# A graph attention kernel: the gathers of a pair of batches in one run, with a wait for their landing between pairs

## The reference

```python
q = (feat @ Wq.T + bq).reshape(n, H, HD)
k = (feat @ Wk.T + bk).reshape(n, H, HD)
v = (feat @ Wv.T + bv).reshape(n, H, HD)
score = jnp.einsum('ehd,ehd->eh', q[edge_dst], k[edge_src])
score = jnp.clip(score / math.sqrt(HD), -10.0, 10.0)
...
alpha = ex / den[edge_dst]
wv = jax.ops.segment_sum(alpha[:, :, None] * v[edge_src], edge_dst, num_segments=n).reshape(n, C)
y = wv @ Wp.T + bp
x = feat + y
h = _layernorm(x, ln_g, ln_b)
h = jax.nn.gelu(h @ W1.T + b1, approximate=False) @ W2.T + b2
return x + h
```

## Time and profile before

| | us |
|---|---|
| median of 3 runs | 1454.29 (1449.91 to 1466.74) |
| the profiled execution | 1484.0 |
| TensorE busy | 1135.0 |
| VectorE busy | 954.9 |
| GpSimd busy | 912.0 |
| ScalarE busy | 672.3 |
| GpSimd idle before gathers | 443.4 |
| VectorE idle before products | 346.6 |

### The profile page before, as it was taken

One profiled execution on the slowest core, in us unless ns is written; L12 is line 12 of the kernel. 1 busy time (PEld: TensorE's weight loads), 2 busy tenths in 40 slices (PEclk: granted clock), 3 DMA queues, 4 the chain that ended last, 5 costly groups with the idle time before them and its releaser, 6 DMA issues.

```text
span 1484.0 us, 26187 instructions
## 1 busy us (share of the span) xinstructions
PE 1135.0 (76%) x6188; PEld 724.7 (49%) x6188; DVE 954.9 (64%) x1539; ACT 672.3 (45%) x1936; POOL 912.0 (61%) x1550
## 2 busy tenths in 40 slices
PE   8956778776977778777866876768877967877887
PEld 6823335454544454444544544544544544544566
DVE  6806676677676576666666666657667657666573
ACT  3212235455544545535544544535544535544543
POOL 4584667677776566766667566666667566666500
PEclk9976668999898788888798788887897788878699
DMA  9985877768777667776677676676677676676510
GB/s 328 314 253 178 254 227 225 229 199 253 214 220 225 203 188 222 227 232 196 197 237 208 191 230 197 199 236 179 206 236 209 191 238 196 197 225 199 180 54 23
DMA packets 154887, 312.25 MB, mean 210 GB/s; under 512 B 32200, under 2 KB 73126, under 8 KB 154791
## 3 DMA queue, kind: packets, MB, share of 16 engines
q0 software_dynamic: 61536, 200.85, 45.6%
q1 hardware_dynamic: 93254, 110.43, 23.3%
HBM read 270.02 MB, written 41.16 MB: 210 GB/s over the span
## 4 chain that ended last, share of the span: by engine, by line
PE 42%; another core or an unknown queue 23%; ACT 14%; issue 14%; DVE 5%; ACTq 1%; DVEq 0%; DMA 0%; SPq 0%
PE bank L483 9%; PE bank L503 7%; PE bank L951 5%; PE quad L875 4%; PE bank L930 3%; PE quad L942 3%; PE bank L977 3%; PE bank L964 2%; ACT hid L496 2%; PE bank L455 2%; ACT hid L491 1%; DVE kv L1636 1%; ACT hn L1276 1%; ACT staged L1217 1%
## 5 line engine op out<-in xcount | busy, mean ns | idle before, releaser
L401 POOL DMA_INDIRECT kv<-kv_rows,src_sb x750 | 721.5, 962 | 443.4 <-PE bank L951 212.1
L1616 DVE TENSOR_TENSOR prod<-kv,quad 128x1024 f32<-128x1024 f32 x196 | 239.3, 1221 | 346.6 <-remote 228.0
L1636 DVE TENSOR_TENSOR kv<-kv,bank 128x1024 f32<-128x1024 f32 x196 | 238.2, 1215 | 16.7 <-ACT kv L1209 16.7
L1623 DVE TENSOR_REDUCE score<-prod 128x32 f32<-128x1024 f32 x196 | 237.7, 1213 | 0.8
L483 PE MATMUL bank<-hT,w_sb 128*128 128x256 f32 x736 | 212.4, 440 | 17.9 <-ACT hid L491 17.9
L951 PE MATMUL bank<-kv,onehot 128*32 128x264 f32 x1568 | 150.1, 442 | 83.2 <-issue 49.5
L503 PE MATMUL bank<-w_sb,hid 128*128 128x256 f32 x736 | 205.3, 435 | 0.9 <-issue 0.7
L483 PEld LDWEIGHTS bank<-hT,w_sb 128*128 128x128 f32 x736 | 159.6, 222 | 52.5 <-issue 11.6
L942 PE MATMUL quad<-qwin,onehotT 32*128 32x256 f32 x1568 | 108.8, 354 | 95.7 <-issue 54.1
L503 PEld LDWEIGHTS bank<-w_sb,hid 128*128 128x128 f32 x736 | 159.8, 223 | 34.5 <-issue 8.7
L930 PE MATMUL bank<-staged,place 128*128 128x264 f32 x196 | 81.5, 502 | 113.8 <-ACT staged L1217 76.0
(11 more groups left out here) (164 smaller groups left out, 1421.0 us busy)
## 6 DMA issues: line engine op xcount, KB each, us to landing
qwin<-q_rows SPq DMA_DIRECT2D x392, 64.0 KB
dst_rows<-edge_dstT SPq DMA_DIRECT2D x50, 256.0 KB
q_rows<-q_next SPq DMA_DIRECT2D x25, 512.0 KB
kv_rows<-kv_out SPq DMA_DIRECT2D x24, 512.0 KB
kv<-kv_rows,src_sb POOLq DMA_INDIRECT x750
agg_rows<-acc_sb SPq DMA_DIRECT2D x98, 82.5 KB
xT_sb<-xT SPq DMA_DIRECT2D x25, 256.0 KB, 5.4
xq_sb<-xT SPq DMA_DIRECT2D x25, 256.0 KB
```

The lines of the kernel that those rows point to most:

```text
L401: return nc.gpsimd.indirect_dma_start(out=rows, out_offset=None, in_=kv_dram, in_offset=bass.IndirectOffsetOnAxis(ap=index, axis=0))
L1616: nc.vector.tensor_tensor(prod[:, slot % 2].rearrange("p (i c) -> p i c", c=C), kv[:, slot, :, 0:C], quad[:, :, 0:C], ALU.mult).then_inc(s ...
L1623: nc.vector.tensor_reduce(score[:, slot % 2], prod[:, slot % 2].rearrange("p (h d) -> p h d", d=HD), AX.X, ALU.add).then_inc(s_score, 1)
L1636: nc.vector.tensor_tensor(kv[:, slot, :, C:2 * C].rearrange("p i (h d) -> p i h d", d=HD), kv[:, slot, :, C:2 * C].rearrange("p i (h d) -> ...
```

## The change

The iotas behind the gathers are gone, with their tile and semaphore. The waits stand now only in front of an even batch, that is of a pair: GpSimd waits until all gathers of the two batches before have landed (`last_pair_landed`), and until both batches of the pair that held the slots have been added up. Then it issues the gathers of both batches in a row.

```diff
-            def pause(parity, t, last):
-                done = nc.gpsimd.iota(idle_rows[:, parity, t], [[1, PAUSE]], base=0, channel_multiplier=0,
-                                      allow_small_or_imprecise_dtypes=True)
-                if last:
-                    done.then_inc(s_pause, 1)
+            def last_pair_landed(turn, i):
+                for b in range(2):
+                    slot = (i - 2 + b) % SLOTS
+                    pool.wait_ge(s_kv[slot], kv_done(turn if i else turn - 1, slot))
+                    pool.sem_inc(s_gate_pool, 1)
 
             def edges(turn, r, parity):
                 for i in range(SLOTS):
...
                     if i % 4 == 0:
                         pool.wait_ge(s_src[buffer], 16 * (r + 1))
-                    if exists(n - SLOTS, BATCHES):
-                        pool.wait_ge(s_part, n - SLOTS + 1)
+                    if i % 2 == 0 and exists(n - 2, BATCHES):
+                        last_pair_landed(turn, i)
+                    if i % 2 == 0 and exists(n - SLOTS, BATCHES):
+                        pool.wait_ge(s_part, n - SLOTS + 2)
                         pool.sem_inc(s_gate_pool, 1)
-                    if exists(n - 2, BATCHES):
-                        pool.wait_ge(s_pause, n - 1)
-                        pool.sem_inc(s_gate_pool, 1)
-                    tiles = gathered(n) - len(x_tiles(turn, i))
-                    for t in range(tiles):
+                    for t in range(gathered(n) - len(x_tiles(turn, i))):
                         col = (i % 4) * TILES + t
                         gather_rows(kv[:, i, t, 0:2 * C], src_sb[:, buffer, col:col + 1]).then_inc(s_kv[i], 16)
-                        pause(i % 2, t, t == tiles - 1)
```

More of the change, by code:

```diff
@@ L17 @@
 WIN = 32
-PAUSE = 64
 WINDOW_STARTS = (0, 10, 25, 41)
@@ L161, in gnn_program @@
         onehotT = sb("onehotT", [P, 4, 2 * P], f32r)
-        idle_rows = sb("idle_rows", [P, 2, TILES, PAUSE])
         onehot = sb("onehot", [P, 4, PAIR_TILES, WIN])
@@ L264, in gnn_program @@
         s_xkvm = sem("x_rows_projected")
-        s_pause = sem("pauses_done")
         s_ohT = sem("transposed_onehots_ready")
```

## The result

The kernel after took **1478.65 us** (median; 1475.99 to 1482.76) where the kernel before took 1455.09 beside it: a ratio of 1.0248, with a 95% interval of 1.018 to 1.0316. The forecast was 1424 us and faster. The time lies inside the range given (1375 to 1482), the sign is wrong.

What follows compares the result with a forecast made beforehand. It took TensorE's signals, held up while GpSimd issues gathers, to bound the kernel. Terms -16 - 8 - 8 - 8 + 10 = -30 us took the median 1454.29 to 1424 us; own range 1395 to 1442, wider range 1375 to 1482.

Steps and rivals of the forecast that it cites:

- What bounds the kernel: No engine is full; TensorE's signals come late while GpSimd issues gathers, behind 23% unknown time (341 us) in the chain.
- The iotas go, -16 us: Inside pairs on GpSimd: 46 us less issuing at 0.35 us per us, -16 us (0 to -46).
- The wait for landing, and its floor: Between pairs on GpSimd: landing 2.1 us, waking 0.9, so a 12.3 us cycle under the present 13.6 a pair.
- The lead of 13 us as cover: Gathers start over 13 us ahead of their products, which was to cover later starts and landing waits at no cost.
- The start, -8 us: First run of 27 gathers is broken up, so first products come earlier than 115.69: -8 us (0 to -18).
- Long runs broken, -8: Runs of eleven gathers, as around 1065, can't occur any more: -8 us (0 to -20).
- fewer runs, -8: 98 runs of gathers instead of 114 to 120, each ending with up to 1 us without signals: -8 us (0 to -22).
- The wait for both batches of the old pair, 0: Even batch's gathers start 5 to 7 us later, with the odd one's slot; covered by the lead, so 0.
- Runs of eight, +10: Runs of eight gathers instead of four and four may hold signals up longer: +10 us (0 to +80).
- landing is exposed: Rival, chance 0.03: lead used up, 206 us of landing on the path less the iotas' 154: +52, 1506 us.

Runs made afterwards that it cites:

- g3: Kernel before with iotas of 256 columns instead of 64, with late signals: 1372.7 us, 0.9202 of before.
- f1: Kernel before unchanged, run again for a second profile, with prompt signals: 1152.6 us.
- D: Set of kernels measured side by side with late signals: before took 1493.5 us, four experiments 0.9202 to 0.9936 of it.
- f2: Kernel after unchanged, run again with prompt signals and profiled: 1480.47 us, 1.2863 of before.
- h1: Kernel after unchanged, run once more in another comparison with prompt signals: 1479.25 us, 1.2845 of before.
- A: The comparison that gave the result, with late signals: before 1455.1 us, after 1.0248 of it.
- e3: Kernel after with landing waits only ahead of batches 2, 4 and 6 of the first turn, prompt signals: 1113.6 us, 0.9678 of before.
- e1: Kernel after without its landing waits, with prompt signals: 1102.6 us, 0.9602 of before.
- e6: Kernel before without its iotas and the wait on them, slot wait per batch kept, prompt signals: 1098.6 us, 0.9554 of before.
- k1: Kernel after without its landing waits, with late signals: 1477.4 us, 0.9887 of before.
- g4: Kernel before without its iotas and the wait on them, with late signals: 1476.7 us, 0.9917 of before.
- F: Set measured side by side with late signals: before 1494.7 us, after 0.9935 of it, after without landing waits 0.9887.
- f3: Kernel after with its landing wait moved one pair back, to the pair before last, prompt signals: 1102.3 us, 0.9576 of before.
- B: Set of kernels measured side by side with prompt signals: before took 1150.1 us, four experiments 0.9554 to 1.3213 of it.

## Why the prediction was wrong, point by point

- **What bounds the kernel.** Right for the trace that was read: signals are late because of the gathers (g3). But their lateness is a condition of the comparison and not of the kernel (f1), and one profile could not show that.
- **The iotas go, -16 us.** Right in size with late signals, as far as D can tell: -12 to -17 us, and the interval of the ratio reaches from -7 to -18 us. The spacing is 1.26 us as taken. With prompt signals the rate is 1 us per us of issuing and not 0.35: -51.5 us.
- **The wait for landing, and its floor: the step that failed.** The prediction worked out GpSimd's own cycle as 9.3 + 2.1 + 0.9 = 12.3 us a pair, found it under 13.6, and so took the wait as hidden. Waking is 0.93 us as taken. Landing is 3.18 us (after) to 3.28 us (f2) after the end of a run of eight, not 2.1; the 2.1 were read off the DMA share after one run at the start, and a share that has fallen is not the last landing of a run in the steady state. In the trace of before the last landing recorded in a break came 2.4 us after the run (mean of the 111 breaks over 1.5 us after 130 us), so only a part of the missing 1.1 us could be read in advance. The cycle is 13.66 us. Over 98 pairs that is 133 us, and the floor of the whole kernel rises from some 1350 to 1480 us: over the 1424 forecast, and over the 1455 of before. f2 and h1 show this floor where signals are prompt (1480.5 and 1479.3 us). After took the same 1478.65 in A, and its trace there has 396.3 us of waits for landings against 19.2 for slots: GpSimd's own cycle set its pace. The comparison was also made with the profiled turns, 54.4 us, of an execution 30 us over its median; per pair the median's pace is 0.3 us less, 13.3, so even the pace to be beaten was nearer.
- **The lead of 13 us as cover.** It was there, and was spent: a cycle longer than the pace eats any lead. In the profile of after the last recorded landing of a batch is a median 3.5 us ahead of its products, where it was 21.0 before. A lead covers a delay once, not one in every pair.
- **The start, -8 us.** The first products came at 93.16, even earlier than the 99 hoped for. The first 27 gathers have gone out by 126.9 instead of 115.0, but in the kernel before the next three wait for slots, and the 30th ends at 135.1 in after and at 136.3 before; the products of batch 8 start 11.6 us earlier in after. So with late signals the gain was there at that point, though the pace of later pairs decides what it is worth, and it wasn't measured by itself. With prompt signals the same break costs 11 us (e3).
- **Long runs broken, -8, and fewer runs, -8.** Not borne out: signals are late inside the shorter, regular runs too (5.96 us of idleness in the break shown above), by a median of 4.4 us where it was 3.3. They come 1.65 us after a run's last gather (median of those over 1 us late), where the forecast had 0.3 to 0.7 and at most 1. The products' waits for "remote" grew to 346.9 us, in 88 places instead of 53; how much of that costs time isn't shown, as GpSimd's cycle is the longer path (f2's products wait 428.8 us for their gathers at the same total time).
- **The wait for both batches of the old pair, 0.** Right: at most 4 us (e1 against e6), nothing seen between k1 and g4, which ran in two comparisons (0.9887 and 0.9917).
- **Runs of eight, +10.** No support: nothing seen (k1 against g4, runs of 7.7 against 5.3).
- **The rivals.** What happened is "landing is exposed", given 0.03, in another form than priced: it is not that 2.1 us a pair lie on the path, but that GpSimd's whole cycle becomes the path. The Trainium skill ("DMA: Bandwidth & Descriptors", section "Rules for kernel authors") has the rule that this breaks: issue early, wait late. The runs agree with it, 1102 us without the wait and 1480 with it where signals are prompt. By the rule of "SBUF — State Buffer", section "Who interferes with whom", which the Trainium skill states for ports, TensorE waits on no one. No row here shows ports; in f1 its signals come 0.03 us after its q rows, which fits, but the earlier trace rows and g3 show that they can be late all the same.

What stays open: the size of the parts in comparison A itself. There before took 1455 us and after 1.0248 of it, in F 1495 and 0.9935. After differs by 0.4% between the two and before by 2.7%, so the sign hangs on how much the late signals cost the kernel before. With late signals the landing wait cost only 6.6 us in F, and without it the kernel still took 1477 us there; so that the wait is the whole loss is shown for prompt signals alone, and for A it is argued from the floor. That the kernel without the landing wait would have been near 1440 us in A (0.9887 of before) is an estimate from F, not a measurement. Nor is it known what makes signals late in one comparison and prompt in another.

**The better kernel** is the one with half of the change: no iotas, no landing waits. It is faster than before in both kinds, with late signals by less than 1% (e6 and g4: 0.9554 and 0.9917). Longer iotas win more with late signals (0.9202) and lose with prompt ones (1.1038).

## What to carry to other kernels

Before a wait is put on an engine that issues transfers, add up that engine's whole cycle (issuing, landing in the loaded state, waking) and compare it with the pace of the kernel; take the landing from a place in the steady state and let it err upward, for a cycle that is 2% too long costs 2% of the whole span: at 54 us a turn that is 1.1 us, and a lead of 13 us is used up in a dozen turns. Wait for a landing one step older if a bound on outstanding transfers is wanted: with prompt signals it costs nothing (f3). And where a profile has unknown releasers, take a second profile of the same kernel at another time before pricing a microsecond by it.

## What the runs showed of the hardware that was not expected

- The same program takes 1150 us in three comparisons and 1455 to 1495 us in three others, each reproducible within one comparison (1147.9 to 1151.9 us in seven runs of B; 1478.9 to 1508.9 in 22 of D). The gathers take the same time in both, 0.96 us; what differs is when the other engines' signals arrive while they are issued: 0.03 us after the q rows' end in f1 (median), 3.3 us in the first profile, a tenth of them over 7.2. SyncE's register moves take 29 ns at the median in both, and a tenth of them over 0.5 us in the late kind.
- With late signals a longer pause after each gather (0.53 instead of 0.37 us) makes the whole kernel 8% faster (g3). The signals stay late, but 95 of 149 come before the run of gathers ends instead of 34 of 102.
- The last gather (128 rows of 2 KB) of a run of seven or eight landed 3.18 us (after) to 3.28 us (f2) after GpSimd was done with it, on the mean; a tenth of them took over 5.25 us in f2.
- With the landing waits TensorE's clock is lower: the granted clock is 0.845 in f2 and 0.935 in f1, and the 736 matmuls of the first feed-forward line (L480 in after, L483 before) take 463 ns instead of 397 on the mean.
